# Edge sort of a four-layer graph network: groups of four chunks handled at once, with four record buffers

## The chip, the cores and the metric

The kernel runs on one core of a Trainium2 chip. Its time is that of one whole execution on the device, in microseconds (us); lower is better. The engines are TensorE (PE, its weight loads PEld), VectorE (DVE), ScalarE (ACT), GpSimd (POOL), which computes nothing here but issues the indirect transfers, and SyncE (SP), which issues the plain ones.

## The reference

The program runs four graph layers over 3125 nodes with 128 features and 103125 edges. What is kept here is what touches the edges; the change lies wholly in the step that puts them in order.

```python
edge_index = jnp.stack([src, dst])                     # 103125 edges
# layer 3: per-edge score terms, 8 heads
scores = einsum(q[src], k[tgt]) / 4 + edges @ We + be  # edges: [103125, 64]
scores = scores * cons[tgt]
scores = scores + relu(distances @ Wd1 + bd1) @ Wd2 + bd2   # distances: [103125, 1]
# layer 2: a scale by edge type
attn = attn * rel_scale[edge_rel] / np.sqrt(DH)        # 16 types, 8 heads
# every layer
jax.ops.segment_sum(message, dst, num_segments=3125)
```

The kernel sorts the edges by destination itself, since all segment sums then run over blocks of 128 nodes. With each edge it stores a record of 26 numbers: source, destination within its block, and three times eight terms (`edges @ We + be`, the distance term with `bd2`, and `rel_scale` of the type).

## The kernel before

`sort_edges` is a counting sort. Edges lie in NC = 806 chunks of 128, one edge a partition. A destination is split into a high part (its block, 25 of them, `NB`) and a low part (128 values). It has three blocks of code, each a program per engine:

1. The histogram (L376 to L403): VectorE makes one-hot matrices of 13 chunks at a time, TensorE adds their products into `hist[low, high]`.
2. The starts (L406 to L460): prefix sums of the histogram give `start[low, high]`, the place of the first edge of each node.
3. The placing (L463 to L661), which is where most of the sort's time goes. It works in groups of G = 4 chunks (512 edges); there are 202 groups, the last with two chunks. What follows calls a group a step. Two sets of buffers (`j` = 0, 1) alternate.

In a step of the placing:

- SP loads, for the four chunks, the keys as rows broadcast to all partitions (`krow`, `lrow`, L501 and L502), the edge attributes (`raw`, L252), the distances as a row broadcast to 16 partitions (`drow`, L259) and the types likewise (`trow`, L262).
- VectorE builds one-hots (`one_hots`, L524 to L530): `hot_lo` and `hot_hi` for counting, `hot_lo_t` for looking up, and for each chunk `inside`, how many earlier edges of the same chunk have the same key. `hot_types` (L280) writes a one-hot of the types into `stack`. The one-hots of a step wait for the third count of the step before (L523).
- TensorE holds a running table in PSUM bank 0. For each chunk in turn: ScalarE copies the table to `run` (L622), TensorE adds the chunk's counts (L597), transposes one chunk of attributes of the next step (L301), and looks up each edge's row of the table with `hot_lo_t` (L602). After the four it multiplies `stack` with the term weights (L312, four products).
- ScalarE besides copies the source and low key into the record (L626), having waited till the scatters that last used the record buffer have landed (`sent[j][g]`), computes the distance term's hidden layer (L329) and moves the transposed attributes (L332). All of this is one queue in that order: L626 of a step stands ahead of L622 of the next.
- VectorE picks each edge's entry of the looked-up row (`positions`, L538, four of them with an accumulator read each), adds `inside`, adds the padding offset, splits the place into a partition and a chunk, and forms `pos` (L545 to L552). `keep` (L285) then adds the biases to the terms and puts them into the record.
- GpSimd scatters 128 records by `pos`, four scatters a step (L649).

On VectorE the order is: `keep` of step s-1, one-hots of step s+1, `positions` of step s, as L563 to L582 write it out. All of the later layers read the records; nothing of them runs until the sort is done.

Of the kernel before, what the change touches and what calls it, by code (L numbers as in the profile page):

```python
# [21 lines left out]
i32 = mybir.dt.int32  # L22
# [173 lines left out]

class EdgeTerms:

    G = 4
    PAIRS = NC // (2 * G)
    TAIL_CHUNKS = NC - (2 * PAIRS + 1) * G
    TAIL_EDGES = E - (2 * PAIRS + 1) * G * P
    HID0, TYPE0 = ATTR, 96
    HID1 = HID0 + HID_D  # L210
    K = TYPE0 + TYPES

    def __init__(self, nc, k, c, a, out, ps):
        G, K = self.G, self.K
        self.nc, self.k, self.a, self.out, self.ps = nc, k, a, out, ps
        self.raw = c.sb("attr_raw", [P, 2, G, ATTR])
        self.drow = c.sb("dist_rows", [P, 2, G * P])
        self.trow = c.sb("type_rows", [P, 2, G * P], i32)
        self.stack = c.sb("stack", [K, 2, G * P])
        self.weight = c.sb("term_weight", [K, 3 * H])  # L220
# [3 lines left out]
        self.bias = c.sb("term_bias", [P, 3, H])  # L224
        self.zeroed, self.weights = c.sem("zeroed"), c.sem("term_weights")
        self.arrived = [c.sem(f"attr_in{j}") for j in range(2)]
        self.rows_in = [c.sem(f"term_rows_in{j}") for j in range(2)]
        self.types_in = [c.sem(f"term_types_in{j}") for j in range(2)]
        self.hots, self.hidden = c.sem("type_hots"), c.sem("dist_hidden")
        self.turned, self.moved = c.sem("attr_turned"), c.sem("attr_moved")  # L230
        self.done, self.kept = c.sem("terms_done"), c.sem("terms_kept")
        self.admitted, self.let = c.sem("loads_admitted"), c.sem("turns_admitted")


    def load_weights(self, sp):
        a, HID0, HID1, TYPE0, K = self.a, self.HID0, self.HID1, self.TYPE0, self.K
        sp.wait_ge(self.zeroed, 4)
        sp.dma_start(self.weight[0:HID0, 0:H], a["L3_gnn_We"]).then_inc(self.weights, 16)
        sp.dma_start(self.weight[HID0:HID1, H:2 * H], a["L3_gnn_Wd2"]).then_inc(self.weights, 16)
        sp.dma_start(self.weight[TYPE0:K, 2 * H:3 * H], a["L2_gnn_rel_scale"]).then_inc(self.weights, 16)  # L240
        sp.dma_start(self.wd1[HID0:HID1, :], a["L3_gnn_Wd1"].rearrange("o p -> p o")).then_inc(self.weights, 16)
        sp.dma_start(self.bd1[HID0:HID1, :], a["L3_gnn_bd1"].rearrange("(p o) -> p o", o=1)).then_inc(self.weights, 16)
        sp.dma_start(self.bias[:, 0, :], a["L3_gnn_be"].rearrange("(o h) -> o h", o=1).to_broadcast([P, H])).then_inc(self.weights, 16)
        sp.dma_start(self.bias[:, 1, :], a["L3_gnn_bd2"].rearrange("(o h) -> o h", o=1).to_broadcast([P, H])).then_inc(self.weights, 16)

    def load(self, sp, i, j, whole=True):
        G, n = self.G, self.G * P if whole else self.TAIL_EDGES
        at = (i * (2 * G) + j * G) * P
        sp.wait_ge(self.turned, i * 2 + (j + 1))
        sp.sem_inc(self.admitted, 1)  # L250
        if whole:
            sp.dma_start(self.raw[:, j, :, :], self.a["edge_attr_64"][ds(at, n), :].rearrange("(c p) f -> p c f", p=P)).then_inc(self.arrived[j], 16)  # L252
        else:
            for q in range(self.TAIL_CHUNKS):
                w = min(P, n - q * P)
                sp.dma_start(self.raw[0:w, j, q, :], self.a["edge_attr_64"][at + q * P:at + q * P + w, :]).then_inc(self.arrived[j], 16)
        sp.wait_ge(self.hidden, i * 2 + (j + 1))
        sp.sem_inc(self.admitted, 1)
        sp.dma_start(self.drow[self.HID0:self.HID1, j, 0:n], self.a["edge_weight1"][ds(at, n), :].rearrange("p o -> o p").to_broadcast([HID_D, n])).then_inc(self.rows_in[j], 16)  # L259
        sp.wait_ge(self.hots, i * 2 + (j + 1))  # L260
        sp.sem_inc(self.admitted, 1)
        sp.dma_start(self.trow[self.TYPE0:self.K, j, 0:n], self.a["edge_type_16"][ds(at, n)].rearrange("(o p) -> o p", o=1).to_broadcast([TYPES, n])).then_inc(self.types_in[j], 16)  # L262


    def begin_vector(self, dve):
        nc = self.nc
        dve.sem_inc(self.hots, 2)
        dve.sem_inc(self.kept, 1)
        nc.vector.memset(self.weight[:, :], 0.0).then_inc(self.zeroed, 1)
        nc.vector.memset(self.bias[:, :, :], 0.0).then_inc(self.zeroed, 1)  # L270
        nc.vector.tensor_scalar(self.type_of[:, :], self.k["part"][:, :], float(-self.TYPE0), None, ALU.add).then_inc(self.zeroed, 1)
        nc.vector.memset(self.stack[self.HID0:self.TYPE0, :, :], 0.0).then_inc(self.zeroed, 1)
        dve.wait_ge(self.zeroed, 4)
        dve.wait_ge(self.weights, 112)

    def hot_types(self, dve, i, j, whole=True):
        n = self.G * P if whole else self.TAIL_EDGES
        dve.wait_ge(self.types_in[j], i * 16 + 16)
        dve.wait_ge(self.done, i * 2 + (j + 1))
        self.nc.vector.tensor_scalar(self.stack[self.TYPE0:self.K, j, 0:n], self.trow[self.TYPE0:self.K, j, 0:n],  # L280
                                     self.type_of[self.TYPE0:self.K, 0:1], None, ALU.is_equal).then_inc(self.hots, 1)

    def keep(self, dve, i, j, n=G):
        dve.wait_ge(self.done, i * 2 + (j + 3))
        self.nc.vector.tensor_tensor(self.out[:, j, 0:n, 2:W_REC], self.ps[:, 1, 0:n * 3 * H].rearrange("p (g w) -> p g w", g=n),  # L285
                                     self.bias[:, :, :].rearrange("p k h -> p (k h)")[:, None, :].to_broadcast([P, n, 3 * H]),
                                     ALU.add).then_inc(self.kept, 1)


    def begin_tensor(self, pe):  # L290
        pe.sem_inc(self.turned, 2)
        pe.sem_inc(self.done, 2)
        pe.wait_ge(self.weights, 112)

    def turn(self, pe, i, j, q, n):

        if q == 0:
            pe.wait_ge(self.arrived[j], i * 16 + 16 * (1 if n == self.G else self.TAIL_CHUNKS))
            pe.wait_ge(self.moved, i * 2 + (j + 1))
            pe.sem_inc(self.let, 1)  # L300
        product = self.nc.tensor.transpose(self.ps[0:ATTR, 6 + j, q * P:(q + 1) * P], self.raw[:, j, q, :], self.k["ident"][:, :])  # L301
        if q == n - 1:
            product.then_inc(self.turned, 1)

    def multiply(self, pe, i, j, q, n):

        if q == 0:
            pe.wait_ge(self.moved, i * 2 + (j + 3))
# [2536 lines left out]
```

## Time and profile before

| | us |
|---|---|
| median of 3 runs | 8057.35 |
| lowest and highest | 8053.37, 8061.86 |
| the profiled execution's own time | 8061.98 |
| its span | 8060.2 |
| first scatter of the sort starts | 221.79 |
| last scatter of the sort starts | 1385.19 |

The profile gives, per engine, busy time, and for each group of instructions of one line the mean duration, the idle time of the engine just ahead of them and what ended it. "issue" is idle time that no wait explains. Times in the timeline are from the start of the span.

### The profile page before, as it was taken

How to read it: one execution, taken by the hardware profiler on the slowest of the kernel's cores; microseconds unless marked ns; L12 is line 12 of the kernel's file. 1: busy time of each engine (PE TensorE's matmuls, PEld its weight loads, DVE VectorE, ACT ScalarE, POOL GpSimd, SP SyncE). 2: the span in 40 equal slices, each digit the busy share in tenths (PEclk: the TensorE clock that was granted, in tenths of full speed). 3: DMA queues.
4: the chain of work that ended last, by engine and by line, in shares of the span. 5: the costliest groups of instructions: out<-in, count | busy, mean ns of one | idle time of the engine just before them, and what ended most of it. 6: DMA issues, size and time to landing. Idle time of an engine off the chain costs nothing. (4 is left out here: it accounts for less than half of the span.)

```text
span 8060.2 us, 144412 instructions
## 1 busy us (share of the span) xinstructions
PE 5681.0 (70%) x31732; PEld 4609.5 (57%) x31872; DVE 4911.6 (61%) x16813; ACT 1400.6 (17%) x3612; POOL 5196.1 (64%) x4817
## 2 busy tenths in 40 slices
PE   2677776588888788887789898668787874555533
PEld 1666665366766577666455554457787763333322
DVE  7788886377776577776555555346666653444454
ACT  0333333022222111111122222100000010000000
POOL 0666666277777377776388888537777733777751
PEclk6555555799999899998899999866766675555556
DMA  1444444444444244444255554324444423333320
GB/s 63 111 112 111 111 111 122 132 129 128 129 128 126 77 129 128 129 129 106 41 83 79 81 80 78 68 68 118 120 120 120 120 47 72 84 85 85 84 57 26
DMA packets 929159, 791.00 MB, mean 98 GB/s; under 512 B 580951, under 2 KB 748307, under 8 KB 927667
## 3 DMA queue, kind: packets, MB, share of 16 engines
q0 software_dynamic: 264032, 434.24, 22.8%
q1 hardware_dynamic: 649788, 342.32, 16.9%
q10 hardware_dynamic: 15264, 13.50, 0.7%
q8 instruction: 40, 0.66, 0.0%
q14 instruction: 35, 0.29, 0.0%
HBM read 700.00 MB, written 88.28 MB: 98 GB/s over the span
## 5 line engine op out<-in xcount | busy, mean ns | idle before, releaser
L1005 POOL DMA_INDIRECT there<-table_wide,idx x1664 | 1624.8, 976 | 780.2 <-issue 553.8
L1906 POOL DMA_INDIRECT there<-table_wide,idx x832 | 918.7, 1104 | 449.2 <-issue 253.2
L1586 POOL DMA_INDIRECT partial_sums<-row_sums1a,idx1a x632 | 1015.6, 1607 | 229.8 <-issue 202.5
L2342 POOL DMA_INDIRECT there<-table_narrow,idx x832 | 802.7, 965 | 478.4 <-issue 235.9
L1094 PE MATMUL ps<-here,hot_t 128*128 x3328 | 1003.2, 427 | 77.1 <-DVE there L1045 60.3
L649 POOL DMA_INDIRECT rec<-out_recd,posd x806 | 804.5, 998 | 389.6 <-issue 215.2
L1102 PE MATMUL ps<-relu,hot_s 128*128 128x128 f32 x3328 | 779.9, 323 | 310.7 <-DVE hot_s L1034 308.8
L1102 PEld LDWEIGHTS ps<-relu,hot_s 128*128 128x128 f32 x3328 | 579.8, 205 | 496.9 <-issue 465.5
L2422 PE MATMUL ps<-here,hot_t 128*128 x1664 | 506.8, 464 | 502.4 <-DVE prod L2367 444.6
L1519 PE MATMUL ps<-src_hot1a,edge_parts1a 128*128 128x512 bf16 (+1 forms) x4661 | 847.4, 332 | 7.5 <-DVE src_hot1a L1393 0.2
L1045 DVE TENSOR_TENSOR there<-there,ps 128x512 f32<-128x512 f32 x832 | 569.2, 684 | 354.0 <-PE ps L1094 353.4
L2422 PEld LDWEIGHTS ps<-here,hot_t 128*128 128x128 f32 x1664 | 389.4, 320 | 618.3 <-issue 617.8
L1094 PEld LDWEIGHTS ps<-here,hot_t 128*128 128x128 f32 x3328 | 609.0, 204 | 165.5 <-issue 111.9
L1519 PEld LDWEIGHTS ps<-src_hot1a,edge_parts1a 128*128 128x128 bf16 x4800 | 407.2, 98 | 408.8 <-issue 4.4
L1075 ACT ACTIVATE relu<-there 128x256 f32<-128x256 f32 x832 | 346.6, 417 | 1648.7 <-DVE there L1045 1538.6
L1034 DVE TENSOR_SCALAR hot_s<-iota,loc,att 128x128 f32<-128x128 f32 x1664 | 520.8, 359 | 133.6 <-ACT att L1077 125.5
L1104 PEld LDWEIGHTS ps<-ones,hot_s 128*128 128x128 f32 x3328 | 546.1, 206 | 0.0
L2070 PE MATMUL ps<-msg,hot_s 128*128 128x128 f32 x1664 | 500.2, 398 | 1.6 <-ACT ps L2028 1.6
L1104 PE MATMUL ps<-ones,hot_s 128*128 128x1 f32 x3328 | 491.4, 217 | 0.0
L602 PEld LDWEIGHTS ps<-rund,hot_lo_td 128*128 128x128 f32 x1612 | 419.3, 324 | 1.2 <-DVE junkd L538 1.2
L1026 DVE SCALAR_TENSOR_TENSOR prod<-there,w_att_w 128x128 f32<-128x128 f32 x1664 | 402.0, 288 | 0.0
L2366 DVE COPY kept<-ps 128x16 f32<-128x16 f32 x416 | 71.5, 172 | 518.5 <-DMA there<-table_narrow,idx 358.5
(413 smaller groups left out, 10470.7 us busy)
## 6 DMA issues: line engine op xcount, KB each, us to landing
locrows<-loc_row SPq DMA_DIRECT2D x416, 256.0 KB, 3.4
krowd<-key_row SPq DMA_DIRECT2D x201, 256.0 KB
src_rows1a<-src_row SPq DMA_DIRECT2D x79, 512.0 KB
there<-table_wide,idx POOLq DMA_INDIRECT x2496, 3.2
lrowd<-lo_row SPq DMA_DIRECT2D x201, 128.0 KB
attr_raw<-in_edge_attr SPq DMA_DIRECT2D x201, 128.0 KB
there<-table_narrow,idx POOLq DMA_INDIRECT x832, 2.5
rec<-out_recd,posd POOLq DMA_INDIRECT x806
```

Of the source, the lines that this page charges most:

```text
L649: nc.gpsimd.indirect_dma_start(rec, bass.IndirectOffsetOnAxis(pos[:, j, g:g + 1], 0), out[:, j, g, :], None).then_inc(sent[j][g], 16)
L1005: nc.gpsimd.indirect_dma_start(there[:, j, q, :], None, table, bass.IndirectOffsetOnAxis(idx[:, j, q:q + 1], 0)).then_inc(gathered[j][q], 16)
L1034: nc.vector.tensor_scalar(hot_s[:, j % 2, q, :], k["iota"][:, :], g["loc"][:, ds(i * CH + (j * U + q), 1)], att[:, j % 2, q:q + 1], ALU.is ...
L1045: nc.vector.tensor_tensor(pair, pair, ps[:, WORK, :], ALU.add).then_inc(summed, 1)
L1094: last = nc.tensor.matmul(ps[:, WORK, (q % 2) * 2 * F:(q % 2 + 1) * 2 * F], hot_t[:, j % 2, q * P:(q + 1) * P], here[:, :, :].rearrange("p ...
L1102: nc.tensor.matmul(wide(ps)[:, ds(blocks[q] * F, F)], hot_s[:, j % 2, q, :], relu[:, j % 2, q, :], start=False, stop=True, skip_group_chec ...
L1104: nc.tensor.matmul(wide(ps)[:, ds(blocks[q] + NP, 1)], hot_s[:, j % 2, q, :], k["ones"][:, 0:1], start=False, stop=True, skip_group_check= ...
L1519: last = nc.tensor.matmul(wide(ps)[:, a:b], edges[:, (j * VISITS + v) % 2, part * F:(part + 1) * F], wide_hot[:, v, a:b], start=opens and ...
L1586: nc.gpsimd.indirect_dma_start(sums[q % TABLES], bass.IndirectOffsetOnAxis(idx[:, j, q:q + 1], 0), out[:, j, q, :], None, compute_op=ALU.a ...
L1906: nc.gpsimd.indirect_dma_start(there[:, j, q, :], None, table, bass.IndirectOffsetOnAxis(idx[:, j, q:q + 1], 0)).then_inc(gathered[j][q], 16)
L2342: nc.gpsimd.indirect_dma_start(there[:, j, q, :], None, table, bass.IndirectOffsetOnAxis(idx[:, j, q:q + 1], 0)).then_inc(gathered[j][q], 16)
L2422: last = nc.tensor.matmul(ps[:, m, (q % 2) * WIDTH:(q % 2 + 1) * WIDTH], hot_t[:, j % 2, q * P:(q + 1) * P], here[:, :, :].rearrange("p t ...
```

## The change

The placing keeps its groups of four chunks and its two sets of one-hot buffers, but does the four at once:

- **Tables.** PSUM bank 0 holds four copies of the running table side by side, preset from `start4`. TensorE adds chunk 0 to copies 1 to 3, chunk 1 to copies 2 and 3, chunk 2 to copy 3, so that they are the tables ahead of the four chunks; ScalarE copies all four at once (128x100 elements); TensorE looks up the four chunks, and then adds what each copy lacks.
- **Places.** One VectorE product of the four looked-up rows with `hot_hi`, one sum over 27 columns (25 of them, `inside`, and a column holding 2^23, to which padding is added in the last step only), two splits and `pos`.
- **Edge terms.** Distances and types of the four chunks lie on 64 partitions each, so `stack` is 128x128 and one product of 96 columns replaces four; attributes are transposed two chunks at a time (128x128) and multiplied two chunks at a time (48 columns, twice). The biases are rows of the weights, so ScalarE copies the terms into the record and `keep` is gone from VectorE. Distances and types are loaded for two steps at once, in four transfers each.
- **Records.** `out` and `pos` have four slots (`SLOTS`), and the wait for landed scatters is for those of four steps ago. The loops run over four steps a turn.
- **Set-up.** Term weights are zeroed by GpSimd and loaded by SP during the histogram block. VectorE's one-hots wait for `added`, the end of TensorE's work on the step two before.

```diff
@@ EdgeTerms
+    HID0, TYPE0 = 0, G * HID_D
+        self.drow = c.sb("dist_rows", [P, 4, P])
+        self.stack = c.sb("stack", [P, 2, P])
     def load(...)
-        sp.dma_start(self.drow[HID0:HID1, j, 0:n], ... .to_broadcast([HID_D, n]))
-        sp.dma_start(self.trow[TYPE0:K, j, 0:n], ... .to_broadcast([TYPES, n]))
+    def load_rows(self, sp, i, h, whole=True):
+        for row, arrived, first, used in ((self.drow, ...), (self.trow, ...)):
+            for g in range(G):
+                sp.dma_start(row[first + g * HID_D:first + (g + 1) * HID_D, 2 * h:2 * h + 2, :], ... .to_broadcast([HID_D, 2, P]))
-    def keep(self, dve, i, j, n=G):
     def turn(...)
+        for pair in range(2 if whole else 1):
+            last = self.nc.tensor.transpose(self.ps[:, 6 + b, pair * P:(pair + 1) * P], self.raw[:, b, 2 * pair:2 * pair + 2, :] ...)
     def multiply(...)
+        self.nc.tensor.matmul(self.ps[:, 4 + b, 0:self.G * TERM], self.stack[:, b, :], self.w_rest[:, :], start=True, stop=False)
+        for pair in range(2 if whole else 1):
+            last = self.nc.tensor.matmul(self.ps[:, 4 + b, ...2 * TERM columns], self.attr_t[:, b, pair * P:(pair + 1) * P], self.w_attr[:, :], start=False)
@@ sort_edges, starts
+                nc.vector.tensor_copy(start4[:, :]..., start[:, None, :].to_broadcast([P, 4, NB]))
@@ placing, vector
+                def ahead(i, j, n):
+                    dve.wait_ge(added, i * 4 + (j + 1))
+                    ... hot_lo, hot_hi -> hots; hot_lo_t -> hots; 4 x inside -> found[..., NB]
+                    terms.hot_types(dve, i, j, n == G)
-                        last = nc.vector.scalar_tensor_tensor(junk[...], iota, hi_col[...], ps[:, 2 + (j * G + g) % 4, 0:NB], ..., accum_out=base[...])
-                    nc.vector.tensor_tensor(base, base, inside, ALU.add)
-                    nc.vector.tensor_tensor(slot, base, pad_col, ALU.add)
+                    nc.vector.tensor_tensor(found[:, b, 0:n, 0:NB], ps[:, 2 + b, 0:n * NB]..., hot_hi[:, b, 0:n, :], ALU.mult)
+                    nc.vector.tensor_reduce(slot[:, b, 0:n], found[:, b, 0:n, :], AX.X, ALU.add)
+                with dve.Fori(1, QUADS) as i:
+                    for j in range(SLOTS):
+                        ahead(*((i, j + 1) if j + 1 < SLOTS else (i + 1, 0)), G)
+                        positions(i, j, G, True)
@@ placing, tensor
+                def step(i, j, n, after):
+                    for g in range(n - 1):
+                        done = count(b, g, g + 1, n - 1)
+                    terms.turn(pe, *after)
+                    terms.multiply(pe, i, j, kept, n == G)
+                    pe.wait_ge(copied, i * 4 + (j + 1))
+                    for g in range(n):
+                        done = nc.tensor.matmul(ps[:, 2 + b, g * NB:(g + 1) * NB], hot_lo_t[:, b, g, :], run[:, b, g, :])
+                        for g in range(n):
+                            done = count(b, g, 0, g)
@@ placing, scalar
+                    nc.scalar.activation(run[:, b, 0:n, :]..., ps[:, 0, 0:n * NB], ACT.Copy)
+                    terms.fill(act, *after)
+                            act.wait_ge(sent[j][g], i * 16)
+                    nc.scalar.activation(out[:, j, 0:n, 0:2], keys[...], ACT.Copy)
+                    act.wait_ge(terms.done, i * 4 + (j + 3))
+                    nc.scalar.activation(out[:, j, 0:n, 2:W_REC], ps[:, 4 + b, 0:n * 3 * H]..., ACT.Copy)
```

TensorE in the placing loop, before: the last chunk's count, transpose and look-up, then the four products of the terms, then the first count of the next step. `ps` is PSUM, `hot_hid` and `hot_lod` the one-hots, `rund` the copied table.

```order
L596 REGISTER_ALU
L597 MATMUL ps<-hot_hid,hot_lod 128x25
L301 MATMUL ps<-ident,attr_raw 64x128
L602 MATMUL ps<-rund,hot_lo_td 128x25
L308 REGISTER_ALU
L312 MATMUL ps<-term_weight,stack 128x24 x4
L596 REGISTER_ALU
L597 MATMUL ps<-hot_hid,hot_lod 128x25
```

TensorE at the same place in the changed kernel, behind the three counts ahead of the copy:

```order
L317 MATMUL ps<-ident,attr_raw 128x128 x2
L323 REGISTER_ALU
L326 REGISTER_ALU
L327 MATMUL ps<-w_rest,stack 128x96
L329 MATMUL ps<-w_attr,attr_t 128x48 x2
L607 REGISTER_ALU
L610 MATMUL ps<-rund,hot_lo_td 128x25 x4
L593 MATMUL ps<-hot_hid,hot_lod 128x25
L593 MATMUL ps<-hot_hid,hot_lod 128x50
L593 MATMUL ps<-hot_hid,hot_lod 128x75
L593 MATMUL ps<-hot_hid,hot_lod 128x100
```

The transposes and the products of the terms now stand between the counts and the look-ups, and the look-ups follow one another without a count or a wait between them.

VectorE in the placing loop, before, behind the four L538: sums, splits, `pos` and `keep`.

```order
L541 REGISTER_ALU
L545 TENSOR_TENSOR based<-based,insided 128x4
L546 ISA
L547 REGISTER_ALU
L547 TENSOR_TENSOR slotd<-based,pad_cold 128x4
L548 REGISTER_ALU
L549 TENSOR_SCALAR placed<-slotd 128x4
L550 TENSOR_SCALAR chunkd<-slotd 128x4
L551 REGISTER_ALU
L552 SCALAR_TENSOR_TENSOR posd<-placed,chunkd 128x4
L284 REGISTER_ALU
L285 TENSOR_TENSOR out_recd<-ps,term_bias 128x4x24
```

VectorE at the same place in the changed kernel, from the type one-hot of the step ahead on:

```order
L306 TENSOR_SCALAR stack<-type_rows,type_of 64x128
L561 REGISTER_ALU
L562 TENSOR_TENSOR foundd<-ps,hot_hid 128x4x25
L563 REGISTER_ALU
L564 TENSOR_REDUCE slotd<-foundd 128x4
L566 TENSOR_SCALAR placed<-slotd 128x4
L567 TENSOR_SCALAR shared<-slotd 128x4
L571 ISA
L572 SCALAR_TENSOR_TENSOR posd<-placed,shared 128x4
```

Five operations stand where there were ten (the four L538 included), and nothing of the terms follows them.

SP in the placing loop, before: one step's transfers.

```order
L501 ISA
L501 DMA krowd<-key_row 128x512
L502 REGISTER_ALU
L502 DMA lrowd<-lo_row 128x512
L249 REGISTER_ALU
L252 ISA
L252 DMA attr_raw<-in_edge_attr 128x4x64
L259 DMA dist_rows<-in_edge_weight 16x512
L262 DMA type_rows<-in_edge_type 16x512
```

SP in the changed kernel, from the last of four distance transfers of an even step to the end of the odd step behind it:

```order
L271 DMA dist_rows<-in_edge_weight 16x2x128
L271 DMA type_rows<-in_edge_type 16x2x128 x4
L259 ISA
L259 DMA attr_raw<-in_edge_attr 128x4x64
L519 REGISTER_ALU
L521 ISA
L521 DMA krowd<-key_row 128x512
L522 REGISTER_ALU
L522 DMA lrowd<-lo_row 128x512
L259 ISA
L259 DMA attr_raw<-in_edge_attr 128x4x64
```

An even step now issues eleven transfers and an odd one three, where every step issued five; the attributes stand last.

## Rows read from the trace of the kernel before

**Rows 1.** the page, costliest groups: line, engine, mean ns, idle before

```profile
L649 POOL DMA_INDIRECT rec<-out_recd,posd x806 | 804.5, 998 | 389.6 <-issue 215.2
```

**Rows 2.** two stretches: us, busy of PE, PEld, DVE, ACT, POOL, PEclk, DMA

```profile
50.00:202.00 152.00, 37.81 (x819) 28.46 (x819) 144.44 (x149) 0.00 (x0) 0.82 (x1) 0.51 0.00 0
600.00:800.00 200.00, 141.76 (x830) 135.22 (x831) 161.79 (x900) 78.14 (x244) 138.15 (x140) 0.50 0.44 111
```

**Rows 3.** line L649: GpSimd idle before its scatters, us and times, until what

```profile
  issue: 215.2, 672
  DVE out_recd L285: 139.8, 117
  ACT out_recd L626: 34.3, 16
```

**Rows 4.** timeline (start, duration) of GpSimd: first and last scatters

```profile
221.79 1.19 POOL L649 DMA_INDIRECT rec<-out_recd,posd  x1 [29.74 <-ACT out_recd L626]
...
1385.19 0.96 POOL L649 DMA_INDIRECT rec<-out_recd,posd  x1 [0.30 <-issue]
```

**Rows 5.** waits over the placing: us in total, times, longest

```profile
ACT out_recd L626 <- DMA rec<-out_recd,posd: 454.2, 200, 3.7
PE ps L597 <- ACT rund L622: 316.7, 200, 3.0
DVE hot_lod L524 <- PE ps L597: 120.8, 146, 2.7
```

**Rows 6.** timeline of the placing, rows of three engines and GpSimd

```profile
599.03 0.21 ACT L626 ACTIVATE out_recd<-keys 128x8 f32 x1 [2.40 <-DMA rec<-out_recd,posd]
...
600.59 0.17 ACT L622 ACTIVATE rund<-ps 128x25 f32<-128x25 f32 x1
...
602.12 0.20 PE L597 MATMUL ps<-hot_hid,hot_lod 128*128 128x25 bf16 x1
...
602.50 0.69 DVE L524 TENSOR_TENSOR hot_lod<-iota,keys 128x512 bf16<-128x512 f32 x1 [0.57 <-PE ps L597]
...
602.64 0.20 PE L597 MATMUL ps<-hot_hid,hot_lod 128*128 128x25 bf16 x1
...
603.16 1.88 PE L312 MATMUL ps<-term_weight,stack 112*128 112x24 f32 x8
...
605.66 0.24 DVE L538 SCALAR_TENSOR_TENSOR junkd<-iota,hi_cold,ps 128x25 f32<-128x25 f32 x1
...
607.71 0.26 DVE L285 TENSOR_TENSOR out_recd<-ps,term_bias 128x96 f32<-128x96 f32 x1 [0.34 <-issue]
...
608.78 1.02 POOL L649 DMA_INDIRECT rec<-out_recd,posd  x1 [0.86 <-DVE out_recd L285]
...
617.02 0.21 ACT L626 ACTIVATE out_recd<-keys 128x8 f32 x1 [3.06 <-DMA rec<-out_recd,posd]
```

**Rows 7.** groups over the first 1400 us: shape, busy, mean ns

```profile
L280 DVE TENSOR_SCALAR stack<-type_rows,type_of 16x512 f32<-16x512 int32 x201 | 119.8, 596 | 6.5
...
L552 DVE SCALAR_TENSOR_TENSOR posd<-placed,chunkd 128x4 int32<-128x4 int32 x201 | 32.8, 163 | 7.6
```

**Rows 8.** a group of VectorE in a later layer, and two of GpSimd

```profile
L1966 DVE TENSOR_REDUCE found_most<-ps 128x1 f32<-128x128 f32 x104 | 29.4, 282 | 0.5 <-PE ps L2062 0.5
L1586 POOL DMA_INDIRECT partial_sums<-row_sums1a,idx1a x632 | 1015.6, 1607 | 229.8 <-issue 202.5 <-DMA partial_sums<-row_sums1a,idx1a 14.6 <-DVE row_sums1a L1381 12.7
L1906 POOL DMA_INDIRECT there<-table_wide,idx x832 | 918.7, 1104 | 449.2 <-issue 253.2 <-DMA idx<-gather 196.0
```

**Rows 9.** timeline of SP in one step: start, duration

```profile
605.05 0.36 SPq L501 DMA_DIRECT2D krowd<-key_row  x1
...
607.42 0.33 SPq L262 DMA_DIRECT2D type_rows<-in_edge_type  x1
```

**Rows 10.** timeline, start of the placing

```profile
205.63 0.35 SPq L501 DMA_DIRECT2D krowd<-key_row  x1
...
211.41 0.82 PE L301 MATMUL ps<-ident,attr_raw 128*64 128x128 f32 x3 [10.82 <-DMA attr_raw<-in_edge_attr]
```

More of the change, by code:

```diff
@@ L356, in sort_edges @@
         start = c.sb("start" + tag, [P, NB])
+        start4 = c.sb("start4" + tag, [P, 4 * NB])
+        terms = EdgeTerms(nc, k, c, a)
         with ExitStack() as ctx2:
@@ L367, in sort_edges, with _ @@
             GC = 13
+            @block.gpsimd
+            def _(pool):
+                terms.clear_weights(pool)
+            @block.sync
+            def _(sp):
+                terms.load_weights(sp)
             @block.vector
@@ L560, in finish @@
-                def finish(i, j, n=G):
-                    terms.keep(dve, i, j, n)
+                    dve.wait_ge(split, i * 8 + (2 * j + 2))
+                    nc.vector.scalar_tensor_tensor(pos[:, j, 0:n], place[:, b, 0:n], NV + 1 - 1.0 / P, share[:, b, 0:n], ALU.mult, ALU.add).then_inc(placed, 1)
                 terms.begin_vector(dve)
                 ahead(0, 0, G)
-                ahead(0, 1, G)
-                positions(0, 0, G, False)
-                finish(0, 0)
-                ahead(1, 0, G)
@@ L582, in _ @@
-                finish(PAIRS, 1, tail)
+                for j in range(SLOTS):
+                    ahead(*((0, j + 1) if j + 1 < SLOTS else (1, 0)), G)
+                    positions(0, j, G, False)
+                with dve.Fori(1, QUADS) as i:
+                    for j in range(SLOTS):
+                        ahead(*((i, j + 1) if j + 1 < SLOTS else (i + 1, 0)), G)
+                        positions(i, j, G, True)
+                ahead(QUADS, 1, tail)
+                positions(QUADS, 0, G, True)
@@ L607, in _ @@
-                terms.begin_tensor(pe)
-                for g in range(G):
-                    terms.turn(pe, 0, 0, g, G)
-                with pe.Fori(0, PAIRS) as i:
-                    for j in range(2):
-                        step(i, j, G, G)
-                step(PAIRS, 0, G, tail)
-                step(PAIRS, 1, tail)
+                pe.sem_inc(added, 2)
+                nc.tensor.matmul(ps[:, 0, 0:G * NB], k["ident"][:, :], start4[:, :], start=True, stop=True, skip_group_check=True)
@@ L616, in _ @@
+                terms.begin_tensor(pe)
+                terms.turn(pe, 0, 0)
+                with pe.Fori(0, QUADS) as i:
+                    for j in range(SLOTS):
+                        step(i, j, G, (i, j + 1) if j + 1 < SLOTS else (i + 1, 0))
+                step(QUADS, 0, G, (QUADS, 1, False))
+                step(QUADS, 1, tail, None)
             @block.scalar
             def _(act):
-                def step(i, j, n, before):
-                    at = i * (2 * G) + j * G
-                    for g in range(n):
-                        act.wait_ge(counted, at + (g + 2))
-                        nc.scalar.activation(run[:, j, g, :], ps[:, 0, 0:NB], ACT.Copy).then_inc(copied, 1)
-                    if before:
+                act.sem_inc(kept, 2)
@@ L641, in _ @@
+                with act.Fori(1, QUADS) as i:
+                    for j in range(SLOTS):
+                        step(i, j, G, (i, j + 1) if j + 1 < SLOTS else (i + 1, 0), True)
+                step(QUADS, 0, G, (QUADS, 1, False), True)
+                step(QUADS, 1, tail, None, True)
             @block.gpsimd
```

393 lines of the change are left out of this document (190 added, 203 removed).

## The prediction, made before the run

> **What bounds the kernel now.** I read the page first. It has one group of the sort among its costliest: the 806 scatters of L649, 998 ns each, with 389.6 us of idle time ahead of them [rows 1]. The change touches the placing alone, and nothing of the later layers can start before it ends, so what counts is how long the placing lasts. The first scatter starts at 221.79, the last ends at 1385.19 + 0.96 = 1386.15 [rows 4]: 1164.4 us, or 5.78 us for each of 201.5 steps of four scatters.
>
> Then the table of stretches. In 200 us in the middle no engine is full: VectorE 161.8, TensorE 141.8 at a granted clock of 0.50 (1.2 GHz), GpSimd 138.2 [rows 2]. So it is a chain with waits, and the waits say which. GpSimd's idle time of 389.6 us [rows 1] is in 672 cases the plain gap between two scatters, 215.2 us, 0.320 us each; 139.8 us end with `keep` (L285) and 34.3 with L626, of which 29.74 is the wait for the first scatter [rows 3, 4]. Those 117 + 16 - 1 = 132 waits of 144.4 us hold 132 x 0.320 = 42 us that the gap would cost anyhow: about 102 us are real waiting. Behind that stands a ring. ScalarE waits 454.2 us, 200 times, for landed scatters; TensorE waits 316.7 us for ScalarE's copy of the table; VectorE 120.8 us for TensorE's count [rows 5].
>
> The timeline shows the ring once round [rows 6]. A landing lets L626 go at 599.03; the fills behind it delay the table copy to 600.59 (1.56 us); the third count starts at 602.12 (1.53); VectorE's one-hots of the next step start at 602.50 (0.38); they end where L538 starts, 605.66 (3.16); `keep` starts at 607.71 (2.05); the scatters start at 608.78 (1.07), and the ScalarE copy that waits for them to land goes at 617.02 (8.24). That is 17.99 us, and it spans three steps: 6.0 us a step here, 5.78 on average. So the two record buffers are what bounds the placing, with ScalarE's single queue carrying the delay into the counts, and GpSimd close behind.
>
> **What the change does to this, part by part.**
>
> Record buffers, two to four. The wait for landings now looks back four steps. Scatters and landing take 8.24 us [rows 6], and four steps of GpSimd alone take over 20, so the wait can still hold ScalarE but no longer hold up GpSimd: the records it releases are due three steps later. GpSimd's real waits go, if nothing else is slower than it.
>
> What is late next: GpSimd itself. Its pitch is 0.998 + 0.320 = 1.318 us [rows 1, 3], 5.27 a step, 806 x 1.318 = 1062 us. From below the bound is the bare scatter at the end of the placing, when VectorE has nothing left to do: 0.96 + 0.30 = 1.26 [rows 4], 1016 us. From above it is the gather L1906, 1104 ns [rows 8], so 1.42 with the gap, 1145 us. I take 1.318, since these are the same scatters beside the same one-hots, which stay as they are. The gain is 1164.4 - 1062 = 102 us, which is the 102 of the waits again.
>
> TensorE must stay under 5.27. The eight passes of the four products L312 take 1.88, 0.235 a pass (a float32 product is two); a chunk's count, transpose and look-up take 0.52 (602.12 to 602.64) [rows 6]. Now: 4 x 0.52 + 1.88 = 3.96 a step. After: look-ups 8 passes, terms 6 in place of 8, 14 x 0.235 = 3.29; two transposes of full width, which I price as a pass each, 0.47; seven counts with 350 columns in all, 0.29 at a column a cycle of 1.2 GHz. Sum 4.05. Two exposed handovers of 0.38 (the one from count to VectorE [rows 6]) make 4.8 at the most. Both ends are under 5.27, so TensorE costs nothing; the four waits for ScalarE's copies become one, covered by the transposes and terms.
>
> VectorE: the one-hots take 3.16 [rows 6]; the type one-hot of 596 ns [rows 7] shrinks from 512 to 128 columns, which I put at half its time, so 2.86. The four L538, the two sums and `keep` leave; in comes a product from PSUM like L285 (0.26 [rows 6]), a sum of 108 elements (282 ns for 128 [rows 8]) and three small operations of 163 ns [rows 7], with two handovers within the engine about 1.2. Sum 4.1, under 5.27 too. The added wait, one-hots of step s+1 for `added` of step s-1, stands ahead of `positions` of step s; what it waits for ends one step earlier than the third count does now. The ring through both engines (`positions`, one-hots of step s+2, its terms and look-ups) is 1.2 + 2.86 + 3.29 + 3 x 0.38 = 8.5 for two steps, 4.25 each.
>
> ScalarE does less: one table copy for four, fills on fewer columns, one copy of the terms added (a product's worth, some 0.26). It is idle for most of the step now and stays so.
>
> SP: five transfers begin within 605.05 to 607.42, about 0.55 each with the gap [rows 9]. A pair of steps now has 14 in place of 10: 7.7 us in 10.5. Eleven stand in the even step (6 us against 5.27), so the odd step's keys come 0.8 us late; they are loaded two steps ahead, and this costs nothing. Bytes are nearly the same, at 0.44 of the transfer engines [rows 2].
>
> Start. Seven weight transfers (7 x 0.55 = 3.9) leave the front of the placing, so the keys are asked for at about 201 and not at 205.63; but attributes now stand behind eight row transfers (4.4 us), and TensorE's queue begins with them (211.41 [rows 10]). I bound the gain by 0 and 8 us and take 4. In the histogram block the 26 weight transfers (14 us) and five fills by GpSimd lie beside VectorE, busy 144.44 of 152 us [rows 2]: 0. The copy to `start4` adds 0.3.
>
> **Sum.** 8061.98 - 102 - 4 + 0.3 = 7956 for the profiled execution. It lies 4.6 above the median of the runs, so 7951.
>
> **Rivals.**
>
> *The feeding engines set the pace.* My sums for TensorE (4.05 to 4.8) and VectorE (4.1) are sums of what is busy, and now they fall 0.5 to 1 us short of what a step takes. Should they come to 5.5 us a step through waits between four engines in step, the placing takes 201.5 x 5.5 = 1108 us, 46 more: 7997. For it: before, a chain no engine filled set the pace. Against: that chain had the landing in it.
>
> *VectorE slows the scatters.* A scatter lasts 0.96 with VectorE idle at the end and 1.19 at the start with its one-hots beside it [rows 4]; gathers L1906 have a mean of 1104 ns [rows 8]. With a step shorter by a tenth, more one-hots fall on each scatter. At 1.42 the placing takes 1145 us, 83 more: 8034. Against: per scatter VectorE does less than before. The Trainium skill, GPSIMD Engine Reference, Key points, says that GpSimd shares its SBUF interfaces with VectorE and contends with instructions in a two-port mode or with two SBUF inputs. By that rule, the trace agrees: the one-hots are of these kinds.
>
> *Scatters queue up, and the kernel is slower.* The place is L661 of the changed kernel. With up to sixteen scatters under way in place of eight, GpSimd may have to wait within a scatter for room. The accumulating scatters L1586 last 1607 ns [rows 8]; at 1.607 + 0.320 = 1.93 the placing takes 1553 us, 491 more than forecast: 8442. It decides from a pitch of 1.45 on, (1164.4 + 4)/806. Against: L1586 does other work per element.
>
> *The four buffers bring no relief,* because the landing is awaited in another way (VectorE's wait ahead of `pos`, ScalarE's ahead of the terms): 8057.
>
> *Bare scatters.* At 1.26 the placing takes 1016, 46 less: 7905.
>
> **Chances.** Forecast, a pitch of 1.28 to 1.35, 7920 to 7977: 75%. Feeding engines 7%, VectorE on the scatters 6%, queueing 4%, no relief 2%, bare scatters 6%. The range takes the forecast, half of the bare scatters and the feeding engines: 7915 to 8000, about 85%. What a measurement can tell from no change is some 0.2%, 16 us. Faster by more: 75 + 7 + 6 + 6 = 94%; within it 2%; slower 4%.
>
> **What would show it.** Right: scatters from about 218 to 1280; next to no waits ahead of them but the gap; mean scatter near 1.0 us; TensorE near 0.8 busy at 0.50; ScalarE still waiting for landings. The step on the ring is wrong if GpSimd still waits for terms or places; the step on TensorE if a step's work exceeds 4.8; the pitch if the scatters' mean leaves 0.96 to 1.03; the start if the first scatter comes after 222. A change in the later layers, or a place of the sort other than the placing, would make the sum wrong.

## The result, and the profile after

The changed kernel takes 7931.45 us, median of 4 runs (7916.64 to 7933.17); the kernel before, on the same chip, 8056.68 (4 runs, 8053.37 to 8061.86). The ratio is 0.984, with a 95% interval of 0.9823 to 0.9857: 125 us less, where the prediction had 7951 and a range of 7915 to 8000.

The page has for the scatters, where [rows 1] stood before:

```profile
L661 POOL DMA_INDIRECT rec<-out_recd,posd x806 | 796.8, 989 | 270.5 <-issue 232.8
```

Idle time before them fell by 119.1 us, and their own by 7.7. The view of that line says what ended the idle time (us, times), and who waited for the scatters; it answers to [rows 3, 5]:

```profile
L661 POOL DMA_INDIRECT rec<-out_recd,posd x806: 954/958/1461, 218.1 to 1259.6; - x162
its engine sat idle before it (us, times) until:
  issue: 232.8, 763
  ACT out_recd L639: 29.8, 17
  ACT out_recd L641: 6.4, 21
  DVE posd L572: 1.5, 5
who waited for it (us, times):
  ACT out_recd L639: 636.3, 174
  DVE posd L572: 145.7, 83
```

Of the 29.8, 24.89 is the wait for the first scatter; nothing but the plain gap, 232.8 / 763 = 0.305 us, is left between scatters. ScalarE now waits longer for landings than before (636.3 us for 454.2) and VectorE waits for them too (145.7 us), and GpSimd waits for neither beyond that gap: the 21 and 5 cases of L641 and L572 are 0.30 us each. The timeline has the first and the last scatter [rows 4]:

```profile
218.13 1.14 POOL L661 DMA_INDIRECT rec<-out_recd,posd  x1 [24.89 <-ACT out_recd L639]
...
1259.63 0.96 POOL L661 DMA_INDIRECT rec<-out_recd,posd  x1 [0.31 <-issue]
```

So the placing takes 1042.5 us, 1.294 a scatter, where it took 1164.4. The profiled executions are 128.8 us apart: 3.7 in the start, 121.9 in the placing, 3.2 behind it. Since the part behind the last scatter differs from execution to execution by more than that (6660 to 6697 us in eight profiled executions, of kernels that have the same code there but for line numbers), the placing, read from the trace, is what the experiments are compared by.

The stretch of [rows 2], 200 us in the middle, after:

```profile
600.00:800.00 200.00, 149.57 (x898) 144.85 (x897) 139.16 (x662) 45.77 (x190) 152.41 (x157) 0.50 0.56 127
```

At 5.17 us a step TensorE is busy 3.87 of it, VectorE 3.60, ScalarE 1.18 and GpSimd 3.94; with its four gaps of 0.305 GpSimd fills the step.

### The profile page after: what moved, and what is told of

It reads as the page before. It is cut to its first block and busy times, and to the rows that moved or that the text cites. A ratio compares the mean times of both kernels' runs of the same rounds, so it can differ in the third digit from the quotient of the medians.

```text
span 7931.5 us, 138403 instructions
## 1 busy us (share of the span) xinstructions
PE 5641.2 (71%) x31668; PEld 4576.7 (58%) x31669; DVE 4694.5 (59%) x15001; ACT 1192.7 (15%) x3210; POOL 5180.7 (65%) x4822
## 5 line engine op out<-in xcount | busy, mean ns | idle before, releaser
L661 POOL DMA_INDIRECT rec<-out_recd,posd x806 | 796.8, 989 | 270.5 <-issue 232.8
L1530 PE MATMUL ps<-src_hot1a,edge_parts1a 128*128 128x512 bf16 x4800 | 867.5, 333 | 0.0
L610 PE MATMUL ps<-rund,hot_lo_td 128*128 128x25 f32 x1612 | 376.7, 386 | 68.6 <-ACT rund L633 51.3
L610 PEld LDWEIGHTS ps<-rund,hot_lo_td 128*128 128x128 f32 x1612 | 365.8, 332 | 74.6 <-issue 74.4
```

Source lines behind the costliest of these rows:

```text
L610: done = nc.tensor.matmul(ps[:, 2 + b, g * NB:(g + 1) * NB], hot_lo_t[:, b, g, :], run[:, b, g, :], start=True, stop=True, skip_group_chec ...
L661: nc.gpsimd.indirect_dma_start(rec, bass.IndirectOffsetOnAxis(pos[:, j, g:g + 1], 0), out[:, j, g, :], None).then_inc(sent[j][g], 16)
L1530: last = nc.tensor.matmul(wide(ps)[:, a:b], edges[:, (j * VISITS + v) % 2, part * F:(part + 1) * F], wide_hot[:, v, a:b], start=opens and ...
```

## The experiments

The table has, of each trace, the placing (start of the first to end of the last scatter), the scatters' mean length and pitch, and the time by which a step's edge terms were in its records before its first scatter began, least and most from the 21st to the 195th step.

| kernel | placing | mean | pitch | terms ready ahead |
|---|---|---|---|---|
| before | 1164.4 | 0.998 | 1.445 | 0.8 to 2.6 |
| after | 1042.5 | 0.989 | 1.294 | 9.3 to 14.6 |
| f1, after again | 1046.4 | 0.994 | 1.299 | 10.9 to 14.5 |
| e1, waits two steps back | 1055.1 | 0.999 | 1.309 | 0.8 to 4.1 |
| e2, before with four buffers | 1054.4 | 1.003 | 1.309 | 1.9 to 2.9 |
| f2, the same again | 1051.7 | 0.999 | 1.305 | 1.9 to 2.8 |
| e6, one more one-hot | 1065.0 | 1.017 | 1.322 | |
| f3, one more PSUM copy | 1054.4 | 1.004 | 1.309 | |
| e3, after, one scatter a step | 946.2 | 1.032 | 4.70 a step | |
| f4, before with four, one scatter | 1005.0 | 0.992 | 5.00 a step | |

**e1: the rework without the buffers.** The changed kernel, in which ScalarE and VectorE wait for the scatters of two steps ago, as before, and not of four.

```diff
+            def two_back(engine, i, j, n):
...
+                for g in range(n):
+                    engine.wait_ge(sent[(j + 2) % SLOTS][g], (i * 16 + 16) if j >= 2 else i * 16)
...
-                            act.wait_ge(sent[j][g], i * 16)
+                    two_back(act, i, j, n)
```

> The changed kernel, with one thing undone: the record copy on ScalarE and pos on VectorE wait for the scatters of two steps ago and not of four, as two record buffers would make them. Theory A, the number of buffers brought the gain: the wait binds again, a step takes 5.5 to 5.8 us as before, the placing 1110 to 1165 us, the kernel 8000 to 8057. Theory B, the shorter chain brought it: with all other work of a step now done ahead of the wait, the ring is landing, 0.5 us of copies, 1.07 to the scatter, 8.24 for scatters and landing, about 9.8 us for two steps, 4.9 each, which is under GpSimd's 5.17; the placing stays at 1042 to 1060, the kernel at 7931 to 7950, and GpSimd waits a little.

**e2: the buffers without the rework.** The kernel before, with `out`, `pos` and `sent` of four slots; L626 and L545 wait for the scatters of four steps ago.

```diff
-            pos = s.sb("pos" + tag, [P, 2, G], i32)
-            out = s.sb("out_rec" + tag, [P, 2, G, W])
+            pos = s.sb("pos" + tag, [P, 4, G], i32)
+            out = s.sb("out_rec" + tag, [P, 4, G, W])
```

> The kernel before, with four record buffers alone: out and pos have four slots, the waits for landed scatters look back four steps; no other work is changed. Theory A, buffers alone bring the gain: real waits of GpSimd (102 us) go, the placing takes 1045 to 1070 us, the kernel 7935 to 7960. Theory B, the work of the step had to shrink as well: VectorE needs 3.16 + 2.05 + 0.26 = 5.47 us a step, over GpSimd's 5.17 to 5.27, so the placing takes 1102 us or more and the kernel 7995 to 8057.

Each brought nearly all of the gain: for e1 theory B held, for e2 theory A. The kernel before took 8052.71 beside them; e1 took 7938.64 (ratio 0.9855, 0.9839 to 0.9872), e2 7941.66 (0.9858, 0.9842 to 0.9875), and both intervals overlap that of the whole change. In e1 the landing is waited for as often as before, for longer, and GpSimd has 10 gaps longer than the plain one, 4.4 us more in all:

```profile
ACT out_recd L641 <- DMA rec<-out_recd,posd: 768.3, 200, 7.8
POOL rec L663 <- issue: 232.1, 756, 0.6
```

In e2 no wait of the placing ends with a landing, and the old work on the chunks, all of it, keeps GpSimd fed, with VectorE and TensorE fuller than in [rows 2]:

```profile
600.00:800.00 200.00, 162.14 (x925) 150.66 (x925) 177.89 (x1001) 86.48 (x269) 153.34 (x153) 0.50 0.53 124
```

Two theories that each gave the gain to one side are both too narrow. The ring of the prediction was the bound, landing and work together, and it gives way at either end: with the landing two steps off, a ring of less work closes before GpSimd is through; with the landing four steps off the old work is short enough. The two causes do not add, since GpSimd's pitch stands behind both.

**f1 and f2: how much of the last 12 us is real.** The changed kernel and e2 a second time, side by side.

> The changed kernel a second time, beside the kernel before with four record buffers on the same chip, to see how much of the 12 us between their placings (1042.5 against 1054.4) is the kernels and how much the execution. If the rework of the chunks' work shortens the scatters, this placing is again 1040 to 1045 us (a pitch of 1.290 to 1.297), and 8 to 15 us shorter than that of the run beside it. If the 12 us were chance, the two differ by less than 5 us, either way.

> The kernel before with four record buffers and nothing else, a second time. Rework shortens scatters: placing 1050 to 1060 us, mean scatter 1.00, 8 to 15 us longer than the changed kernel beside it. Chance: within 5 us of it.

The placings are 5.3 us apart, after 11.9 the first time, which is neither the 8 to 15 of the one theory nor within the 5 of the other: the rework beside four buffers is worth 5 to 12 us in two pairs, nearly all of it in the scatters' length, and more runs would be needed to say which. The whole times are further apart, 7932.49 and 7969.83 (one execution each). 28 us of that lie behind the placing, where the two kernels have the same code. e2's profiled execution, 7973.15, has them too, and its three others don't (7936.50 to 7945.81); what they are stays open.

**e3 and f4: the pace of the feeding engines.** Only the first of a step's four chunks is scattered, so GpSimd has time to spare. Three quarters of the records are missing; the layers behind the sort work on what is there, and their time is not read.

```diff
-                        for g in range(n):
+                        for g in range(1):
```

> The changed kernel with one scatter a step in place of four (three quarters of the records are left out), so that GpSimd is out of the way and the pace is that of the engines that feed it. Forecast: TensorE 4.05 to 4.8 us a step and VectorE 4.1, so the placing takes 820 to 970 us. Rival, the feeding engines were already close behind GpSimd: 5.0 us a step or more, 1010 us or more. If SP with its eleven transfers in every other step, or the attributes that stand last there, set the pace, TensorE's wait for attributes stays as long as it is (192 us).

> The kernel before with four record buffers, scattering only the first of the four chunks of a step, so that GpSimd is never the bound and the placing shows at what pace the old work of the other engines feeds it. Three quarters of the records are missing, and the later layers' time means nothing; only the placing is read. The same cut in the changed kernel gave 946 us, 4.70 a step. Theory A, the rework gives the feeding engines margin: 980 to 1040 us here, 4.85 to 5.17 a step, still under GpSimd's 5.2. Theory B, the old work was as slow as GpSimd: 1045 or more. Theory C, the rework gives no margin: 935 to 960.

The reworked engines deliver a step in 4.70 us, the old ones in 5.00, against the 5.17 to 5.24 that GpSimd takes; both came out within their forecasts. The granted clock was 1.00 in e3's placing and 0.50 in f4's, but that is not the difference: TensorE's groups last as long at either level (last section). The margin is real but small, and in e3 TensorE waits for attributes almost as long as in the changed kernel (182.4 us), now with no GpSimd behind it to cover them. The rows are of e3's waits:

```profile
PE ps L317 <- DMA attr_raw<-in_edge_attr: 187.5, 124, 3.4
ACT attr_t L344 <- PE ps L317: 184.3, 125, 3.4
DVE foundd L562 <- PE ps L610: 153.9, 109, 3.4
```

**e6 and f3: what more work on VectorE does to the scatters.** The changed kernel with one unused VectorE operation a step behind the type one-hot: in e6 a one-hot of 128x512 from two inputs in SBUF, in f3 a copy of 128x512 from PSUM. Both take 0.69 us.

```diff
+                    nc.vector.tensor_tensor(spare[:, 0:n, :], k["iota"]..., lo_col[...]..., ALU.is_equal).then_inc(spared, 1)
```

```diff
+                    nc.vector.tensor_copy(spare[:, 0:n, :]..., ps[:, 1, 0:n * P]).then_inc(spared, 1)
```

> The changed kernel with one more VectorE one-hot a step (128x512, 0.69 us, into a tile that nobody reads), behind the type one-hot. VectorE has room: 4.1 + 0.6 = 4.7 us of 5.17. Theory, VectorE's operations with two inputs lengthen the scatters beside them: a scatter's mean is 0.989 against 0.958 bare, with some 2.3 us of one-hots a step; 30% more of them add 0.009 us a scatter, 5 to 15 us in all, and the mean goes to about 0.998. Rival, they don't: mean 0.989, the same time within 3 us. If the feeding engines were the bound, 100 us or more.

> The changed kernel with one more VectorE operation a step, a copy of 128x512 from PSUM to bf16 in SBUF, in the place where an earlier run had a one-hot of 128x512 with two SBUF inputs. The output is unchanged; the copy is read by nobody. Theory A, it is the two SBUF inputs that lengthen scatters: mean scatter stays at 0.98 to 0.995 us and the placing within 5 us of the changed kernel's own on this chip, where the one-hot gave 1.017 and 1065. Theory B, any VectorE work beside a scatter lengthens it, or the added work delays the places: placing 12 to 25 us longer, mean 1.01 or more.

The one-hot lengthened the placing by 22.5 us over the changed kernel's first run and 18.5 over its second (its whole time was 7955.74, ratio 0.988, 0.9863 to 0.9896), the copy by 12.0 and 8.0. For the one-hot that is the theory's sign, but more than its 5 to 15 us and a mean of 1.017 where it said 0.998. No wait was added to GpSimd in either. f3 met neither theory: more than nothing, less than the one-hot. The means hide what happens; single scatters show it.

## When a scatter is long

With all 806 scatters of the changed kernel laid over VectorE's rows, 169 last 1.0 us or more, and 168 of them have one thing in common: one of the operations for the step ahead was already running when the scatter began. These are `hot_lo` (L546), `hot_hi` (L548), `hot_lo_t` (L550) and the four of `inside` (L552, `junk` in the rows). Where one of them had begun 0.10 us or more before the scatter and ran on for more than 0.14 us of it, the scatter ended 0.81 to 0.85 us after that operation did: in all 180 cases of the changed kernel, all 205 of f1, all 194 of e1, and 216 of 217 in the kernel before. The lowest share of the eight placings is f2's, 144 of 149. An undisturbed scatter lasts 0.957 us, so one that ends 0.83 after an operation is longer than that only if the operation lasts past its first 0.13 us. The two left over are the first scatters of their placings. In the kernel before, the second scatter (1.12) fits the type one-hot L280 in the same way, and nine of 1.00 have L280 begin 0.38 or 0.39 us into them. The timeline shows a case of each of two lines (start, duration):

```profile
290.87 0.69 DVE L546 TENSOR_TENSOR hot_lod<-iota,keys 128x512 bf16<-128x512 f32 x1 [0.58 <-issue]
291.15 1.25 POOL L661 DMA_INDIRECT rec<-out_recd,posd  x1 [0.30 <-issue]
```

```profile
399.12 0.35 DVE L552 SCALAR_TENSOR_TENSOR junkd<-krowd,key_col,before 128x128 f32<-128x128 f32 x1
...
399.22 1.08 POOL L661 DMA_INDIRECT rec<-out_recd,posd  x1 [0.30 <-issue]
...
399.77 0.29 DVE L306 TENSOR_SCALAR stack<-type_rows,type_of 64x128 f32<-64x128 int32 x1
```

The first scatter ends at 292.40, 0.84 after L546; the second at 400.30, 0.83 after L552. Over 0.957 us the scatters have an excess of 25.7 us in all, and 25.0 of it lies on such cases: 9.2 on 48 scatters behind L546, 7.3 on 65 behind L552, 6.8 on 69 behind L550 and 1.7 on 23 behind L548.

What counts is which of the two began first. Of the same operations, none of the 130 that began between 0.02 us ahead of the scatter and 0.10 behind its start has that distance. Between 0.09 and 0.03 us ahead it goes either way (21 of 52), and where the scatter isn't held, VectorE is: L550 takes up to 0.54 us there for 0.48, L552 0.39 for 0.35. The type one-hot L306, which always stands beside the scatters behind L552, is not what holds them: in the kernel before it (L280) takes 0.74 us there, outlasts the scatter, and all 84 of these scatters last 1.06 to 1.08 as well.

```profile
604.23 0.35 DVE L530 SCALAR_TENSOR_TENSOR junkd<-krowd,key_col,before 128x128 f32<-128x128 f32 x1
604.33 1.07 POOL L649 DMA_INDIRECT rec<-out_recd,posd  x1 [0.30 <-issue]
...
604.88 0.74 DVE L280 TENSOR_SCALAR stack<-type_rows,type_of 16x512 f32<-16x512 int32 x1
```

e6 and f3 separate the kinds. Where e6's one-hot, two inputs in SBUF, had begun 0.5 us before a scatter and ran on for 0.18 of it, all 103 scatters lasted 1.01 to 1.04; where f3's copy from PSUM did, all 92 lasted 0.95 to 0.97. One of e6, then one of f3:

```profile
400.96 0.69 DVE L560 TENSOR_TENSOR spare_hotd<-iota,keys 128x512 bf16<-128x512 f32 x1
401.47 1.02 POOL L667 DMA_INDIRECT rec<-out_recd,posd  x1 [0.30 <-issue]
```

```profile
403.09 0.69 DVE L560 CAST spare_hotd<-ps 128x512 bf16<-128x512 f32 x1
...
403.60 0.96 POOL L666 DMA_INDIRECT rec<-out_recd,posd  x1 [0.30 <-issue]
```

Where e6's one-hot began within a scatter, some 0.3 us after its start, both kept their length: 79 scatters of 0.958 on average, and 0.69 us for the one-hot. So the copy of f3 holds up no scatter itself. Its placing is 8 to 12 us longer because it shifts the others: `hot_lo` held 90 scatters there, 22.5 us in all, against 48 and 9.2 in the changed kernel and 68 and 13.5 in f1. In e6 it held 99 (26.3 us), beside the 104 (6.6 us) of the added one-hot. The last two numbers for the changed kernel, 9.2 and 13.5, also show how much the meeting of the two engines varies from one execution of the same code to the next.

VectorE is held for longer than those 0.06 us too, late in a scatter. In e2 the small L550 (`place`) takes 0.17 us, but 0.41 or 0.42 in 30 of 115 cases between 400 and 1000 us, and all 30 end 0.02 to 0.04 us before a scatter does:

```profile
610.23 0.96 POOL L660 DMA_INDIRECT rec<-out_recd,posd  x1 [0.30 <-issue]
...
610.75 0.42 DVE L550 TENSOR_SCALAR placed<-slotd 128x4 int32<-128x4 int32 x1
610.82 0.35 DVE L551 TENSOR_SCALAR chunkd<-slotd 128x4 int32<-128x4 int32 x1
...
611.50 0.96 POOL L660 DMA_INDIRECT rec<-out_recd,posd  x1 [0.30 <-DVE posd L553]
```

With one scatter a step (f4) L280, L550 and L551 have means of 486, 170 and 162 ns, with four (e2) 562, 234 and 214 (400 to 1000 us): 0.2 us a step that the scatters take from VectorE. This would explain why e2's record is ready by the same 1.9 to 2.9 us through 175 steps though no wait in its trace ties VectorE to GpSimd, and why the old work, 5.00 us a step by itself, was not faster than GpSimd beside it; no run isolates that.

The Trainium skill, SBUF — State Buffer, "SBUF: two separate sides", describes a pair of ports for which VectorE and GpSimd take an exclusive lock for a whole instruction, whichever of them starts first; VectorE takes it in its two-port modes or with two SBUF inputs, the latter only against a GpSimd operation that reads SBUF. By that rule, the trace agrees on who waits, the one that began later, and on the kinds as far as e6 and f3 test them, two SBUF inputs against PSUM. It disagrees on "whole": a one-hot that begins 0.3 us into a scatter is not held, so the scatter does not keep VectorE out for all of its 0.957 us. Why it keeps out a small `tensor_scalar` at 0.5 us but not a one-hot at 0.3 is open.

## Transfers in another order

Four more kernels ran on a chip where every kernel was slower, the kernel before at 9738.81 us (9667.52 to 9778.83), so they are compared with each other alone. They are the changed kernel itself (e0), one whose attributes are asked for right behind the keys, ahead of the distances and types (e4), the same with one scatter a step (e7), and f3's edit (e10).

> The changed kernel once more, for how well the length of the placing repeats from one execution to the next: 1042 us from the first scatter to the end of the last in the first trace. If the length repeats within 3 us, the 12 us by which two buffers alone or four buffers alone stay behind (1055 and 1054) are real; if it comes out between 1050 and 1056, they are not.

> The changed kernel with SP's order changed: an even step's attributes are loaded ahead of its eight transfers of distances and types and not behind them. Theory, GpSimd is the bound and TensorE's waits for attributes (192 us) are covered: the placing stays within 3 us of the changed kernel's, and only the first scatter comes earlier, by 1 to 4 us. Rival, those waits cost something in between: the placing gets 10 us or more shorter.

```diff
                     for j in range(SLOTS):
                         load(i, j, G)
+                        terms.load(sp, i, j)
                         if j % 2 == 0:
                             terms.load_rows(sp, i, j // 2)
-                        terms.load(sp, i, j)
```

> As the run with one scatter a step (three quarters of the records are left out; 4.70 us a step, TensorE waiting 187 us for attributes), with the attributes loaded ahead of distances and types. Theory, SP's order sets the pace of the feeding engines: waits for attributes fall under 60 us and a step takes 4.1 to 4.4 us. Rival, the ring through TensorE and VectorE sets it: 4.6 to 4.7 us as before.

> The run with one more one-hot a step, with a plain copy from PSUM of the same size in its place (128x512, one input, not from SBUF, about 0.65 us a step of VectorE). The extra one-hot took the scatters' mean from 0.989 to 1.017 us and the placing from 1042 to 1065. Theory, it is the two inputs from SBUF that hold up the scatters: mean 0.985 to 0.995, placing 1040 to 1048. Rival, any VectorE work of that length does it: mean about 1.015, placing about 1065.

The changed kernel took 9575.74 there, e4 9588.45, e10 9608.41, with placings of 1342.7, 1349.9 and 1350.1. Each has 105 to 108 long gaps ahead of its scatters, 287 to 312 us in all, which the same kernels don't have elsewhere, and no difference between them can be trusted. Nor can e10 answer what it was made for, which is why f3 repeats it. e7, e4's order with one scatter a step, gave 4.42 us a step against the 4.70 of e3 (the granted clock was 1.00 in both), and TensorE waited 131.9 us for attributes against 187.5. That meets neither of its theories, waits under 60 and 4.1 to 4.4, or 4.6 to 4.7 as before, but speaks for a margin to be had from the order of the transfers. That a disturbed run came out faster makes it likely, but the pair ran on different chips, and at GpSimd's pace the margin buys nothing.

## Why the prediction was right, step by step

- **The ring and the buffers.** Right. The waits of 102 us are gone, and e2 and e1 show that the ring gives way at either end. What the prediction did not say is that the rework alone would do: it costed the other parts only to see that they stay under GpSimd's pitch, and never asked what the old buffers would do with them. Its own numbers held it: 17.99 us for three steps, less 1.56 for the fills ahead of the table copy, 0.30 for the one-hots and 0.85 for the places, is 15.3, under the 15.8 of GpSimd.
- **GpSimd next, at 1.318.** The mechanism is right, the term mis-sized: 1.294, which is 1062 - 1042.5 = 19.5 us. The profiled execution was forecast 23 us too long, 7956 for 7933; another 3.2 lie behind the placing, where it had no change. That 7951 misses the median by no more than 20 is in part luck: the median lies 1.7 us below the profiled execution and not 4.6. The gap went in at 0.320 from [rows 3], but among the 672 of "issue" 33 were longer than 0.35 and held 10.2 us of waits without a name; without them it is 0.305, as after. That is 12 us. The other 7.6 are the scatters, 0.989 for 0.998, and half of that is chance: f1, the same kernel again, has 0.994, and the same gap. The rows of VectorE say what moves the mean. `hot_lo` held 70 scatters of the kernel before, 15.5 us in all, 48 and 9.2 in the first run of the changed kernel, 68 and 13.5 in the second.
- **TensorE.** Its passes came out at 4.64 a step for 4.05: look-ups 1.87 as said, terms 0.58 + 0.98 for 1.41, transposes 0.69 for 0.47, counts 0.52 for 0.29. A busy time of 3.87 shows that they overlap; it stayed under 5.17, so the error cost nothing.
- **VectorE.** 3.60 busy for a sum of 4.1 with its handovers. The type one-hot takes 289 ns, about half of 596 as taken (of which some 110 were VectorE held by scatters, by the 486 of f4); the product 262 and the sum 266. The timeline of a step:

```profile
602.25 0.26 DVE L562 TENSOR_TENSOR foundd<-ps,hot_hid 128x100 f32<-128x100 f32 x1
602.54 0.27 DVE L564 TENSOR_REDUCE slotd<-foundd 128x4 f32<-128x108 f32 x1
602.84 0.17 DVE L566 TENSOR_SCALAR placed<-slotd 128x4 int32<-128x4 int32 x1
602.92 0.16 DVE L567 TENSOR_SCALAR shared<-slotd 128x4 f32<-128x4 f32 x1
...
604.59 0.16 DVE L572 SCALAR_TENSOR_TENSOR posd<-placed,shared 128x4 int32<-128x4 int32 x1 [1.51 <-DMA rec<-out_recd,posd]
```

  From L562 to the end of L567 are 0.83 us; `pos` then waits for a landing, with 7 to 14 us to spare to its scatter (21st to 195th step).
- **SP.** Right that it costs nothing, wrong in how: the attributes, last in each step's list, come late in 134 of the 202 steps at least, and TensorE waits for them instead of being fed two steps ahead. The cover is GpSimd's pace, and e3 shows the price without it.

```profile
PE ps L317 <- DMA attr_raw<-in_edge_attr: 182.4, 134, 3.4
```

- **Start.** 3.66 us for 4: the keys are asked for at 201.46 instead of 205.63.
- **Rivals.** Feeding engines: their pace alone is 4.70, not 5.5. Queueing: no scatter lasts longer for more of them under way, 0.958 undisturbed. Bare scatters: a pitch of 1.262 would need every scatter to start with none of those operations under way. VectorE slowing the scatters is a real mechanism, but the change did not make more of it: it costs 25.7 us in the changed kernel and 29.6 in f1, where (0.998 - 0.957) x 806 = 33 went before. Four buffers bring relief, as e2 shows by itself.

## What to carry to other kernels

Where a chain of waits runs through a ring of buffers, compute the ring with each of its parts changed alone, since the next bound may be reached by the cheapest of them: here, four buffers in place of two gave 111 of 125 us. Once an engine is the bound with no wait ahead of it, lay its instructions one by one over those of the others; a mean of 0.989 us was some 600 scatters of 0.958 and a tail, each of which another engine's operation had held at its start. Ask then which of the two began first, and take a second execution before reading a difference of a few us. An experiment for the next step is to give L546, L550 or L552 another form, one that leaves the scatters alone; by the 25.7 us it has no more than that to give, and it was not run.

## What the runs showed of the hardware

- A scatter of 128 records keeps GpSimd 0.957 us plus a gap of 0.305. If one of VectorE's one-hots or `inside` operations has begun 0.10 us or more before it and still runs past its first 0.14 us, it ends 0.81 to 0.85 after that operation (180 of 180 in the changed kernel), and lasts 1.46 at most. One that begins after the scatter does not do this (0 of 130), nor does a copy from PSUM (0 of 92). The other way round VectorE's `tensor_scalar` is stretched from 0.17 to 0.42 us until the scatter ends.
- In e3 the row of the same stretch reads a granted clock of 1.00 (2.4 GHz) where the changed kernel's reads 0.50 (1.2 GHz), with TensorE busy 160.89 of 200 us against 149.57. The eight passes of the look-ups take 1.87 us in both, and the next group begins 1.70 us behind their start in e3 and 1.69 in the changed kernel (from 599.68 and from 599.93 us). From the transposes on, the terms' two groups and the look-ups begin 0.48, 0.37 and 0.78 us one behind the other in e3, 0.49, 0.37 and 0.78 in the changed kernel. The stretch of e3, then a row of its timeline and the same of the changed kernel's:

```profile
600.00:800.00 200.00, 160.89 (x981) 157.27 (x980) 152.15 (x724) 57.35 (x213) 44.40 (x43) 1.00 0.52 128
```

```profile
599.68 1.87 PE L610 MATMUL ps<-rund,hot_lo_td 128*128 128x25 f32 x8
```

```profile
599.93 1.87 PE L610 MATMUL ps<-rund,hot_lo_td 128*128 128x25 f32 x8
```

  For TensorE's groups of this placing, float32 passes of 25 columns among them, the clock made no difference. The changed kernel itself ran at 0.50 here, the level at which the prediction read its price of 0.235 us a pass.
